# Experts' first two products of the first image moved into the end of the last image; gates spread beside the third products

## The reference

```python
t = t + _L1_attn_ref(_ln_t(t), ...)
t = t + _L1_ffn_ref(_ln_t(t), ...)

def _L1_ffn_ref(x, Wr, br, W1, ..., W2, ..., Wo, bo):
    feat = jnp.mean(x, axis=0)                     # mean over the 8 images
    w = softmax(feat @ Wr + br, axis=-1)           # gates: one weight per token and expert
    h = relu(_bn(x @ W1[e] + b1, ...))             # per expert e
    h = relu(_bn(h @ W2[e] + b2, ...))
    y = h @ Wo[e] + bo
    return sum over e of y[e] * w[:, e]
```

## Time and profile before

| | us |
|---|---|
| median of 3 runs | 3535.88 (3533.53 to 3540.69) |
| the profiled execution | 3533.79, its span 3532.1 |
| PE busy | 3133.6 (89%) |
| ACT busy | 2719.6 (77%) |
| DVE busy | 2047.2 (58%) |
| POOL busy | 288.4 (8%) |
| ACT exponentials of stage D (L920) | 2072.1 in 1536 |
| PE products from the selector (L1309) | 27.5 in 32 records |

### The profile page before, as it was taken

How to read it: one execution, slowest core, us unless ns; L and a number is a source line. 1 busy time by engine, 2 the same in 40 slices (tenths; PEclk the granted TensorE clock), 3 DMA queues, 4 the chain that set the end, 5 groups by cost and what they waited for, 6 DMA issues and landing times.

```text
span 3532.1 us, 71046 instructions
## 1 busy us (share of the span) xinstructions
PE 3133.6 (89%) x27837; PEld 1127.1 (32%) x27837; DVE 2047.2 (58%) x2944; ACT 2719.6 (77%) x2582; POOL 288.4 (8%) x373
## 2 busy tenths in 40 slices
PE   5799999999579898998998998999998988979999
PEld 3344444444122222222222222222222222234443
DVE  3588888888546456556556556556556544422222
ACT  4444444445289999999999999999999999925555
POOL 5100000000211011011011011010011000020000
PEclk9899999999789999999999999999999999969999
DMA  4411221110110210200210210200210211000000
GB/s 180 134 51 46 51 50 36 49 46 18 29 34 17 59 26 19 58 25 18 59 25 17 59 26 17 59 26 17 58 28 17 59 33 27 17 11 9 12 12 15
DMA packets 134481, 136.77 MB, mean 39 GB/s; under 512 B 29103, under 2 KB 113165, under 8 KB 134157
## 3 DMA queue, kind: packets, MB, share of 16 engines
q1 hardware_dynamic: 134156, 132.29, 14.7%
HBM read 70.31 MB, written 55.57 MB: 36 GB/s over the span
## 4 chain that ended last, share of the span: by engine, by line
PE 36%; ACT 35%; issue 19%; DVE 5%; SPq 2%; POOL 2%; DMA 1%; DVEq 0%; ACTq 0%; POOLq 0%
ACT arena L920 34%; PE ps L1248 6%; PE ps L1323 3%; PE ps L1330 3%; PE ps L1335 3%; PE ps L992 3%; PE ps L1039 3%; PE ps L1066 2%; PE ps L1200 2%; PE ps L1041 2%; PE ps L1050 2%; PE ps L1021 2%; DVE arena L1413 1%; SPq L509 1%; DVE arena L1420 1%
## 5 line engine op out<-in xcount | busy, mean ns | idle before, releaser
L920 ACT ACTIVATE arena<-ps 128x1536 f32<-128x1536 f32 x1536 | 2072.1, 1616 | 73.5 <-PE ps L1200 72.6
L1248 PE MATMUL ps<-arena 128*32 128x512 f32 (+3 forms) x12288 | 1275.9, 511 | 1.4 <-DVE arena L1656 1.2
L1656 DVE TENSOR_TENSOR arena<-arena,causal 128x512 f32<-128x512 f32 x1024 | 664.7, 688 | 350.0 <-ACT arena L920 340.4
L1200 PE MATMUL ps<-arena 15*128 15x512 bf16 (+3 forms) x6144 | 615.3, 335 | 198.2 <-ACT arena L920 144.8
L1200 PEld LDWEIGHTS ps<-arena 15*128 15x128 bf16 x6144 | 164.1, 92 | 1139.8 <-ACT arena L920 955.8
L864 ACT ACTIVATE arena<-ps 128x512 f32<-128x512 f32 x512 | 299.7, 595 | 264.3 <-PE ps L1041 253.8
L1248 PEld LDWEIGHTS ps<-arena 128*32 128x32 f32 x12288 | 285.1, 109 | 389.8 <-issue 334.1
L1413 DVE TENSOR_REDUCE arena<-ps 128x32 bf16<-128x1024 f32 x256 | 311.4, 1217 | 119.1 <-PE ps L1021 119.1
L1420 DVE TENSOR_TENSOR arena<-arena,ps 128x512 f32<-128x512 f32 x512 | 329.1, 680 | 24.7 <-PE ps L1050 23.6
L1641 DVE COPY arena<-ps 128x512 f32<-128x512 f32 x256 | 176.6, 690 | 225.1 <-PE ps L1248 224.1
L1039 PE MATMUL ps<-arena 96*128 96x256 bf16 x1024 | 258.0, 277 | 0.3 <-ACT arena L840 0.2
(11 more groups left out here) (195 smaller groups left out, 2020.8 us busy)
## 6 DMA issues: line engine op xcount, KB each, us to landing
arena<-qstack SPq DMA_DIRECT2D x512, 30.0 KB
parts<-arena SPq DMA_DIRECT2D x8, 1536.0 KB, 5.9
arena<-parts SPq DMA_DIRECT2D x48, 256.0 KB, 5.4
arena<-parts SPq DMA_DIRECT2D x96, 128.0 KB, 2.7
arena<-kstack SPq DMA_DIRECT2D x512, 24.0 KB
qstack<-arena SPq DMA_DIRECT2D x48, 192.0 KB, 2.8
attn<-arena SPq DMA_DIRECT2D x512, 12.0 KB
arena<-arena SPq DMA_DIRECT2D x384, 16.0 KB, 1.8
```

Source lines behind the costliest of these rows:

```text
L920: act.activation(PR1[:, at:at + CW], bank(BPC * (f % 2), BPC), ACT.Exp).then_inc(d_exp, 1)
L1200: mm = pe.matmul(bank(at + k)[:, s * P:(s + n) * P], Ks[par][HR * h:HR * h + QROWS, j * P:(j + 1) * P], Qs[par][HR * h:HR * h + QROWS, t * ...
L1248: mm = pe.matmul(o[HR * h:HR * (h + 1), :], V1[n % 2][:, j, v:v + HR], pr[:, h * HALF + s * P:h * HALF + (s + k) * P], start=not opened[hi ...
L1656: dve.tensor_tensor(v, v, m3, ALU.min).then_inc(d_mask, 1)
```

## The change

- TensorE's instructions between the end of stage D and the transposes of the gates get a written order, `TAIL_ORDER`. `f0` to `f16` stand for steps of image 0's experts: `fk` is `first(k)` and `second(k-1)`. The other names are those of the last image's end; `tr` is the transposes, `bias` the gated bias. The last image's steps use banks 4 to 7 only.
- ACT runs the 32 relus of image 0 before the exponential of the router. The results of the second relu go to 16 buffers of their own, `h2_first`, as nothing can consume them before the gates are there.
- The spreading of the gates (`broadcast(e)`) is issued two experts ahead of the third products of image 0, which follow expert by expert, both halves. Its banks rotate over 0-1, 2-3, 6-7, and ACT makes all eight copies to `wB`.
- DVE adds `bias_w` to X, half an image at a time (`biased`), in the place of POOL.
- Images 1 to 7 keep their order; the loop of each engine starts with image 1.

```diff
+TAIL_ORDER = ["f0", "f1", "f2", "f3", "f4", "f5", "f6", "y0", "y1", "f7", "f8", "z0", "z1", "f9", "f10", "m0", "m1", "f11",
+             "f12", "va0", "va1", "f13", "turn", "f14", "w0", "w1", "f15", "lg", "f16", "tr", "bias"]
+TAIL_BANK = {"y0": 6, "y1": 7, "z0": 4, "z1": 5, "m0": 6, "m1": 7, "va0": 4, "va1": 5, "turn": 6, "w0": 7, "w1": 4,
+             "lg": 5, "tr": 6, "bias": 4}
...
+        cut = Cut(in_q)
+        h2_first = [cut([HALF]) for _ in range(6)]
...
+        h2_first += [cut([HALF]) for _ in range(9)]
+        h2_first += [edge]
...
-            pool.wait_ge(f_dve, 8)
-            with pool.Fori(0, B) as i:
-                xi = X[:, ds(i, 1), :].rearrange("p o t -> p (o t)")
-                pool.tensor_tensor(xi, xi, bias_w, ALU.add).then_inc(f_biased, 1)
...
+            def relu1(i, k):
+                n, e = i * (2 * NE) + k, k % NE
+                act.wait_ge(g_h1, n + 1)
+                wait(act, g_h2, n - 1)
+                act.activation(h1[k % 2], bank(k % 2), ACT.Relu, bias=cv(c_B1 + e), scale=cv(c_A1 + e)).then_inc(g_r1, 1)
+
+            def relu2(i, k, to):
+                n, e = i * (2 * NE) + k, k % NE
+                act.wait_ge(g_h2, n + 1)
+                act.activation(to, bank(2 + k % 2), ACT.Relu, bias=cv(c_B2 + e), scale=cv(c_A2 + e)).then_inc(g_r2, 1)
+
+            for k in range(2 * NE):
+                relu1(0, k)
+                if k:
+                    relu2(0, k - 1, h2_first[k - 1])
+            relu2(0, 2 * NE - 1, h2_first[2 * NE - 1])
             act.wait_ge(f_dve, 3)
             act.activation(lw, lg, ACT.Exp).then_inc(f_exp, 1)
-            for e in range(0, NE, 2):
+            for e in range(NE):
                 act.wait_ge(f_wbps, e + 1)
-                act.activation(wB[:, e, :], bank(4, 2), ACT.Copy).then_inc(f_wbA, 1)
+                act.activation(wB[:, e, :], bank((0, 2, 6)[e % 3], 2), ACT.Copy).then_inc(f_wbA, 1)
 
             def act_f(i):
-                def relu2(k):
-                    n, e = i * (2 * NE) + k, k % NE
-                    act.wait_ge(g_h2, n + 1)
-                    wait(act, g_w, n - 1)
-                    act.activation(h2[k % 2], bank(2 + k % 2), ACT.Relu, bias=cv(c_B2 + e),
-                                   scale=cv(c_A2 + e)).then_inc(g_r2, 1)
                 for k in range(2 * NE):
-                    n, e = i * (2 * NE) + k, k % NE
-                    act.wait_ge(g_h1, n + 1)
-                    wait(act, g_h2, n - 1)
-                    act.activation(h1[k % 2], bank(k % 2), ACT.Relu, bias=cv(c_B1 + e),
-                                   scale=cv(c_A1 + e)).then_inc(g_r1, 1)
+                    relu1(i, k)
                     if k:
-                        relu2(k - 1)
-                relu2(2 * NE - 1)
-            peeled(act, B, act_f)
+                        act.wait_ge(g_w, i * (2 * NE) + k - 2)
+                        relu2(i, k - 1, h2[(k - 1) % 2])
...
-            names = list(E_AT.values())
-            for u, name in enumerate(names):
-                if u >= 8:
-                    ED.after(pe, B - 1, E_READ[names[u - 8]])
-                pe_e(B - 1, name, bank(u % 8))
-
-
-            pe.wait_ge(f_dve, 6)
-            for t in range(NT):
-                mm = pe.transpose(bank(2, 2)[0:NE, t * P:(t + 1) * P], lw[:, t, :], ident[:, :])
-            mm.then_inc(f_mm, 1)
-            pe.wait_ge(f_dve, 7)
-            for th in range(2):
-                mm = pe.matmul(bank(2 + th), bo[:, :], wT[0:NE, th * HALF:(th + 1) * HALF], start=True, stop=True)
-            mm.then_inc(f_mm, 1)
-            for e in range(NE):
-                wait(pe, f_wbA if e % 2 == 0 else f_wbV, e // 2)
-                for th in range(2):
-                    mm = pe.matmul(bank(4 + 2 * (e % 2) + th), sel[0:NE, e, :], wT[0:NE, th * HALF:(th + 1) * HALF],
+
+            def first(i, k, y):
+                n = i * (2 * NE) + k
+                wait(pe, g_r1, n - 1)
+                pe.matmul(bank(k % 2), W1[:, k % NE, :], y, start=True, stop=True).then_inc(g_h1, 1)
+
+            def second(i, k):
+                n = i * (2 * NE) + k
+                pe.wait_ge(g_r1, n + 1)
+                wait(pe, g_r2, n - 1)
+                pe.matmul(bank(2 + k % 2), W2[:, k % NE, :], h1[k % 2], start=True, stop=True).then_inc(g_h2, 1)
+
+            for name in TAIL_ORDER:
+                if name[0] == "f":
+                    k = int(name[1:])
+                    if k < 2 * NE:
+                        first(0, k, half(Yall[:, 0, :], k // NE))
+                    if k:
+                        second(0, k - 1)
+                elif name == "tr":
+                    pe.wait_ge(f_dve, 6)
+                    for t in range(NT):
+                        mm = pe.transpose(bank(6, 2)[0:NE, t * P:(t + 1) * P], lw[:, t, :], ident[:, :])
+                    mm.then_inc(f_mm, 1)
+                elif name == "bias":
+                    pe.wait_ge(f_dve, 7)
+                    for th in range(2):
+                        mm = pe.matmul(bank(4 + th), bo[:, :], wT[0:NE, th * HALF:(th + 1) * HALF], start=True, stop=True)
+                    mm.then_inc(f_mm, 1)
+                else:
+                    pe_e(B - 1, name, bank(TAIL_BANK[name]))
+
+            def broadcast(e):
+
+                if e < 3:
+                    pe.wait_ge(g_r1 if e == 0 else g_r2, 2 * NE)
+                else:
+                    pe.wait_ge(f_wbA, e - 2)
+                for th in range(2):
+                    mm = pe.matmul(bank((0, 2, 6)[e % 3] + th), sel[0:NE, e, :], wT[0:NE, th * HALF:(th + 1) * HALF],
                                    start=True, stop=True)
                 mm.then_inc(f_wbps, 1)
-            pe.wait_ge(f_wbA, NE // 2)
-            pe.wait_ge(f_wbV, NE // 2)
-
-            pe.wait_ge(f_dve, 8)
-
+
+            broadcast(0)
+            broadcast(1)
+            for e in range(NE):
+                if e + 2 < NE:
+                    broadcast(e + 2)
+                for th in range(2):
+                    pe.wait_ge(g_w, 2 * e + th + 1)
+                    if e == 0 and th == 0:
+                        pe.wait_ge(f_dve, 8)
+                    pe.matmul(bank(4 + th), Wo[:, e, :], h2w[th], start=e == 0, stop=e == NE - 1).then_inc(g_y3, 1)
+            pe.wait_ge(f_wbA, NE)
...
-            peeled(pe, B, pe_f)
+            with pe.Fori(1, B) as i:
+                pe_f(i)
...
-            for u, name in enumerate(E_AT.values()):
-                dve_e(B - 1, name, bank(u % 8))
+            for name in E_AT.values():
+                dve_e(B - 1, name, bank(TAIL_BANK[name]))
...
-            dve.tensor_copy(bias_w, bank(2, 2)).then_inc(f_dve, 1)
-            for e in range(1, NE, 2):
-                dve.wait_ge(f_wbps, e + 1)
-                dve.tensor_copy(wB[:, e, :], bank(6, 2)).then_inc(f_wbV, 1)
+            dve.tensor_copy(bias_w, bank(4, 2)).then_inc(f_dve, 1)
+
+            def biased(i, th):
+                x = X[:, ds(i, 1), th * HALF:(th + 1) * HALF].rearrange("p o t -> p (o t)")
+                dve.tensor_tensor(x, x, half(bias_w, th), ALU.add).then_inc(f_biased, 1)
+
+            def result(i, th):
+                dve.wait_ge(f_biased, i * 2 + (th + 1))
+                wait(dve, out_stored[th], i * INC)
+                dve.tensor_tensor(res[th], bank(4 + th),
+                                  X[:, ds(i, 1), th * HALF:(th + 1) * HALF].rearrange("p o t -> p (o t)"),
+                                  ALU.add).then_inc(g_res, 1)
+
+            for e in range(NE):
+                dve.wait_ge(f_wbA, e + 1)
+                for th in range(2):
+                    dve.wait_ge(g_r2, NE * th + e + 1)
+                    wait(dve, g_y3, 2 * e + th - 1)
+                    dve.tensor_tensor(h2w[th], h2_first[NE * th + e], half(wB[:, e, :], th), ALU.mult).then_inc(g_w, 1)
+                    if e == 1:
+                        if th == 0:
+                            dve.wait_ge(f_dve, 8)
+                        biased(0, th)
+            for th in range(2):
+                dve.wait_ge(g_y3, 2 * NE - 1 + th)
+                result(0, th)
 
             def dve_f(i):
-                def result(th):
-                    dve.wait_ge(g_y3, (i * 2 + (th + 1)) * NE)
-                    dve.wait_ge(f_biased, i + 1)
-                    wait(dve, out_stored[th], i * INC)
-                    dve.tensor_tensor(res[th], bank(4 + th),
-                                      X[:, ds(i, 1), th * HALF:(th + 1) * HALF].rearrange("p o t -> p (o t)"),
-                                      ALU.add).then_inc(g_res, 1)
                 for k in range(2 * NE):
                     n, th, e = i * (2 * NE) + k, k // NE, k % NE
                     dve.wait_ge(g_r2, n + 1)
-                    wait(dve, g_y3, n - 1)
+                    dve.wait_ge(g_y3, n - 1)
                     dve.tensor_tensor(h2w[k % 2], h2[k % 2], half(wB[:, e, :], th), ALU.mult).then_inc(g_w, 1)
+                    if k in (4, 6):
```

(58 more changed lines are left out.)

1 line of the change is left out of this document (removed).

## The result

The changed kernel takes 3514.63 us (median of 5 runs, 3503.03 to 3517.25) against 3536.14 us (5 runs, 3533.53 to 3540.69) for the kernel before: a ratio of 0.9933, with a 95% interval of 0.9918 to 0.9947. That is faster by 21.5 us of the medians, where 14.4 were forecast. The profiled execution took 3514.63 us, 19.2 less than the 3533.79 of the one before; its span is 3512.9 against 3532.1. The forecast of 3520 had the right sign, and its range held the time.

The account below looks back on a forecast made before the run. Only the last 422 us matter, bound by TensorE idling and products at clock 0.50. Image 0's last third product ends at 3213.7 instead of 3228.1, gaining 14.4 us: 3519.4, given as 3520; range 3498 to 3530, narrower 3516 to 3529.

Parts of the forecast that it names:

- Part 1: Stage D's end to y0: f0 to f6 fill idle TensorE at clock 1.00, y0 at 3121.5 against 3121.15.
- the rival with the fill at 0.50: After stage D the clock falls and interleaved waits keep it down: a loss of 18 us, 3552 us; chance 0.04.
- Part 2: From y0 to va's end: 18 products of 0.86 us plus va, 17.5 us, costing the chain 5.7 us.
- Part 3: From va to the gates' transposes: only f14 charged at 0.50, transposes at 3155.5, chain 7.2 us longer than before.
- Part 4: Gates and image 0's third products: 34 products at 0.50 until the last broadcast, stage ending at 3213.7.
- The rise: Clock's return to 1.00 in the gates stage: only among the last six third products, 4.2 us after they begin.
- A product of the mix: One spreading or third product while both alternate in the gates stage: 1.71 us at clock 0.50.
- The last six third products: End of image 0, no broadcast between: 4.2 us at 0.50, the other 6.0 us shrinking to 3.0.
- the level rises within the mix: Rival: full clock after the first pair of third products, 24 products cheaper by 20.4 us in all, 3502.6 us; chance 0.25.
- The signs that the prediction had set: Last image's end: y0 within 1 us of 3121.5, clock 1.00 from 3110 to 3137, transposes 3155 to 3161, others.
- signs of being wrong: Clock 1.00 in the mix, 0.50 in the fill, y0 later than 3123, or DVE late for third products or in loop.
- Part 5: Work moved to DVE and ACT is covered, perhaps 0.1 to 0.3 us showing at e = 6 and 7; images 1 to 7 unchanged.

Follow-up runs that it names:

- The kernel without the fill: Against the changed kernel, image 0's first and second products are issued after the router's product, not in the gaps; 3528.93 us, ratio 0.9986.
- the two on the loop: Each against the changed kernel: POOL adds the gated bias again, 3518.49 us; ACT's old order of waits restored in the loop, 3518.59 us.
- the kernel with 128 rows: Against the changed kernel, the gate-spreading products read 128 rows instead of 8, the others zeros, bias still 8; 3499.64 us, ratio 0.9898.
- that with 32: Against the changed kernel, the gate-spreading products read 32 rows instead of 8, the others zeros, bias still 8; 3519.67 us, ratio 0.994.

## Why the prediction was right, and where it was off

Stage D ended 2.3 us later in this execution than in the one before (its last copy starts at 3111.57, not at 3109.24), which the change does not touch. The forecasts below are shifted by it.

- **Part 1, the fill before y0.** Forecast: y0 11.5 us behind the first product. Measured: 3123.88 - 3112.37 = 11.51, at a clock of 1.00. Right, and the rival with the fill at 0.50 fell. The kernel without the fill prices the whole overlap at 22 us, the level of the clock in the last image's end included.
- **Part 2, to va.** Forecast 17.5 us for 18 products and va; measured 3139.33 + 1.84 - 3123.88 = 17.3. Right. The twelve products cost the chain their own duration, as the sum had it.
- **Part 3, to the transposes.** Forecast 3155.5, measured 3156.96 - 2.3 = 3154.7. Right to 0.8 us. The assumption that only f14 runs at 0.50 held in this execution: the level fell at 3145.4, was back at 3148.8, and fell again at 3155.7. In the second execution of the same kernel it stayed at 1.00 until 3156.3, so the fall at f14 is one that may or may not come.
- **Part 4, the gates and third products.** From bias to image 1 the forecast was 55.0 us and 48.15 were measured. This is where the step failed, in three terms. *The rise*: it was put behind the last broadcast and came at 3193.2, in the spreading pair ahead of the fourth pair of third products, so that the ten products from this pair on took 9.8 us and not 17.1 (-7.3). *A product of the mix*: 1.71 us was taken from a row of like products behind each other; in the mix a pair takes 3.71, so 1.855 each, which is 1.5 us more over the ten at 0.50. *The last six third products*: 5.84 us (3202.44 to 3208.28) and not 7.2 (-1.4), at 0.97 each, 0.1 above the product itself because of DVE, as the text had feared. Together with 0.3 more for the first eight products they make -6.9.
- **The rival "the level rises within the mix"** thus came half true. It was priced as a rise behind the first pair (24 products, 17.4 us), with a chance of 0.25, while the sum allowed none before the last broadcast. In five executions with 8 rows (the changed kernel twice, the one without the fill, the two on the loop) the rise came 17.4, 33.1, 33.1, 40.3 and 40.5 us behind the start of the bias; the forecast had it at some 52 (28 products of 1.71 and 4.2). A case with the rise in the middle should have stood between the two. How near the total came is in part chance: this one term varies by some 11 us between executions. The signs that the prediction had set say the same: 0.50 until the last broadcast, pairs of 3.41 us and an end of image 0 at 3211 to 3219 did not come. Of its signs of being wrong, DVE's lateness came in the last six third products (0.1 us each), and y0 later than 3123 only through stage D's later end.
- **Part 5.** DVE's and ACT's work is covered, as forecast. "Images 1 to 7 have the same order and the same length" was the one wrong sentence: TensorE's order is the same, ACT's waits are not, and 7 x 0.12 us = 0.8 us followed.

The sum with the measured terms: 14.4 forecast, 6.9 more from part 4, 0.9 from parts 2 and 3, less 0.8 for the loop, make 21.4 against the same stage D; less its 2.3 us, 19.1, where the two profiled executions differ by 19.2.

The rule weighed in part 4 ("TensorE: Matmul & The Clock Gate", section "Why this matters for your kernels", of the Trainium skill) is that a busy TensorE gets the full clock. It is followed by the kernel with 128 rows and not by that with 32, in which TensorE is busy for 39.00 of 39.00 us at 0.50. By the traces it holds here for products that read the whole height. Another rule of the same page, in the Trainium skill's section "The mechanism", says that a weight load overlaps a product in flight only where the row group differs, while a sentence above it there also lets a load run ahead into a background weight buffer. The trace speaks against the "only": between products of 128 rows, whose groups are the same, a pair takes twice 0.86 us, so the load is hidden, and at a change from 8 rows to 128 it isn't.

## What to carry to other kernels

Filling an idle TensorE with independent products ahead of a dependent chain is worth nearly the whole idle time if it keeps the clock, and it also postpones the chain by what is put beside it; both can be summed from a profile to within a microsecond. Where a busy stretch stands at 0.50 in the clock's column, look at the number of rows its products read before reordering anything: here zeros in the unused rows of three experts' operands and the bias took 13 to 17 us off the stretch, all the reordering of the spreading at most 3. When a helper is rewritten, compare the order of its waits too.

## What the hardware showed that was not expected

- **Rows read decide whether products raise the clock.** Products of 8 rows by 512 columns leave it at 0.50 for 27.5 us without a gap, and an even mix of 32-row and 128-row products for 39. With 128 rows, 120 of them zero, the level rises 9.1 us behind the bias's start (3152.96 to 3162.1), and 3.0, 3.3 and 6.2 us behind it with the bias at 128 rows too.
- **An even mix of 8-row and 128-row products holds 1.00 and is slow to reach it**: 19.0 us at 1.00 when entered at 1.00; 19 to 26.5 us at 0.50, and once 4, when entered at 0.50. The rise out of it comes at different points in different executions (17.4 to 40.5 us behind the start of the bias), and why was not found. That chance alone moves the stretch from 40.4 to 51.8 us.
- **The weight load at a change of rows is not hidden.** A pair takes 3.71 us at 0.50 and 1.91 at 1.00 where it takes 3.41 and 1.72 among its like: 0.30 and 0.19 us for each change. The weight loads (PEld) of the changed kernel's first pair of third products show it: 1.50 us idle before the ones at the change, 0.52 before the one among its like:

```profile
3174.07 0.50 PEld L1359 LDWEIGHTS ps<-arena 128*128 128x128 f32 x2 [1.50 <-issue]
...
3175.09 0.34 PEld L1359 LDWEIGHTS ps<-arena 128*128 128x128 f32 x1 [0.52 <-issue]
```

- **The order of two waits on one engine has a price**: each second relu of the loop starts 0.06 us later behind the first, which is 0.12 us for an image, since TensorE waits for it at the head and at the end alone. What the chip does in these 0.06 us is not in the traces and stays open.
